# Eight edge products instead of four behind the aggregation loop of a graph network on one Trainium2 core

## The chip, the core and the metric

The program runs on one core of a Trainium2 chip. A core has five engines that run side by side and wait for each other through semaphores: TensorE (PE, matmuls), VectorE (DVE), ScalarE (ACT), GpSimd (POOL) and SyncE (SP), which issues most of the transfers. All transfers of the core are carried by its 16 DMA engines. The metric is the device time of one execution in microseconds (us). A "tile" is 128 rows of 512 float32 values, 256 KB.

## The reference

Two graph layers with residual and layer norm, on 10,000 nodes of 512 features and 5,000 edges that are sorted by their target node. Only the first layer and the edge term of the second bear on the change:

```python
# layer 0: x is scaled by 1/sqrt(degree) at the source and summed over the edges of each target
norm = dinv[src] * dinv[dst]
H = X @ W
msgs = H[src] * norm[:, None]
out = jax.ops.segment_sum(msgs, dst, num_segments=N) + b
x = _layernorm(x + leaky(out))
...
# layer 1: needs, for each edge, a product of its own attributes with one third of Wr
x_cat = jnp.concatenate([node_feat[src], node_feat[dst], edge_feat], axis=-1)
r = x_cat @ Wr.T + br
```

The kernel sums `dinv[src] * x[src]` over each target's edges first and multiplies by W afterwards. The part `edge_feat @ Wr_edge` depends on nothing of layer 0, so its 40 tile products can stand anywhere ahead of layer 1.

## The kernel before

Edges are cut into 40 tiles (`ET = 40`) of 128. The program is written out in three stages, and the order of the instructions on each engine is the order of its own `..._program` function. There is no scheduler.

**The prologue stage** holds two jobs that share the engines.

The *aggregation* goes over the 40 edge tiles in `NB = 20` turns of two tiles, 2j and 2j+1. For one tile t:
POOL gathers the 128 source rows of x (`x_of`, line 541, into `node_sum`) and their factors (`dinv_of`, line 541, into `dinv_src`); it may run four tiles ahead, since `x_of(t)` waits until tile t-4 has been scaled. ACT scales them (`scale_rows`, line 460, into `acc_x` or `acc_xx`). PE transposes the tile into PSUM (`turn_x`, line 618, four matmuls). DVE runs a segmented prefix sum along the edges (`scan`, line 706, four instructions, into `node_x`). PE transposes back (`turn_back`, line 625), one turn later. ACT scales by the target's factor into one of only two buffers (`sum_rows`, line 466, `sum_y` for even and `sum_xx` for odd tiles), and SP stores it (`store_sums`, line 350, into `sum_table`). `sum_rows(t)` waits until the store of tile t-2 has landed.

The *edge products* are 40 products `edge_part(t)` of 12 matmuls of 128x512 each (lines 208 to 210: float32 as a sum of high and low parts). Their input is loaded by SP (`load_ea`, line 339, four slots), rounded by ACT (`high`, line 449, `ea_hi`), and the rest is taken by DVE (`low`, line 698, `ea_lo`); ACT copies the result out (`part_rows`, line 454, four buffers `part`), and SP stores it (`store_part`, line 346, `edge_part`). The first 11 (`PRE = 11`) stand ahead of the aggregation. `ahead(j)` deals out the rest: 25 to the 20 turns, one to each turn but two to turns 3, 7, 11, 15 and 19, and the last four (`LATE = 4`) behind the loop, in what the code calls turn `j == NB`. Of these four the first stands ahead of the last two `turn_back`, and three behind them.

In a turn PE does `turn_x`, `turn_x`, `edge_part(one)`, `turn_back`, `edge_part(two)` if there is a second, `turn_back`. ACT scales the tiles of the turn after, then `high`, `part_rows`, `sum_rows`. DVE does `scan(2j)`, `low` of the next turn's first edge tile, `scan(2j+1)`, `low` of the next turn's second if there is one. In turns 0 to 5 ACT and DVE also split a half of a later weight each (`weights_high`, line 444, `weights_low`, line 694).

**The node stage** computes layer 0 for 79 node tiles. Before its first tile POOL gathers rows of `sum_table` (line 591, once the last sums have landed), DVE adds them to x (line 1017, `node_agg`), PE transposes (line 1046), writes four banks whole (`open_banks`, line 1028, which waits until all 40 edge parts have been copied out of PSUM), ACT puts the bias into a bank (line 961), ACT and DVE split the transposed tile (lines 945 and 988), and PE multiplies by W (lines 208 to 210 with `agg_hi`, `agg_lo`). From there on one node tile follows another. **The edge stage** and a last stage follow.

The turn behind the loop on SP, before the change:

```python
if j == NB:
    store_sums(2 * j - 2)
    store_sums(2 * j - 1)
    for i in range(R):
        if i == 0:
            sp.wait_ge(back_ok, ET)
        sp.dma_start(g.node_x[:, i, :], g.x[i * P:(i + 1) * P, :])
    for t in ahead(j):
        store_part(t)
    for i in range(R, 2 * R):
        sp.dma_start(g.node_x[:, i, :], ...)
```

Of the kernel before, what the change touches and what calls it, by code (L numbers as in the profile page):

```python
# [263 lines left out]
def prologue_stage(nc, g):  # L264
# [4 lines left out]
    R = 4  # L269
    RP = 4  # L270
    PRE = 11
    LATE = 4
    with ExitStack() as ctx:
        ix = g.index
        run = g.node_x[:, 0:R, :].rearrange("p r (k e) -> p r k e", k=K)
# [59 lines left out]
    def sync_program(sp):  # L335
# [72 lines left out]
        for j in range(NB + 1):  # L408
            one, two = first_and_second(j)
            next_one, next_two = first_and_second(j + 1)  # L410
            if j == NB:
                store_sums(2 * j - 2)
                store_sums(2 * j - 1)
                for i in range(R):
                    if i == 0:
                        sp.wait_ge(back_ok, ET)
                    sp.dma_start(g.node_x[:, i, :], g.x[i * P:(i + 1) * P, :]).then_inc(g.node_in[i], 16)
# [3 lines that stand above are left out]
                    sp.dma_start(g.node_x[:, i, :], g.x[i * P:(i + 1) * P, :]).then_inc(g.node_in[i], 16)  # L421
                continue
            for t in next_one:
                load_ea(t + R)
            if j + 6 < EARLY:
                load_weights(j + 6)
            for t in one:
                store_part(t)
            if j >= 1:
                store_sums(2 * j - 2)  # L430
            for t in next_two:
                load_ea(t + R)
            for t in two:
                store_part(t)
            if j >= 1:
                store_sums(2 * j - 1)

    def scalar_program(act):
        def weights_high(i):
            if i < 2:  # L440
                act.wait_ge(w_in[(0, 4)[i]], 16)
            else:
                act.wait_ge(w_in[i // 2], 32)
            nc.scalar.copy(g.w_half(g.w_hi, i), g.w_half(g.over_lo, i)).then_inc(w_hi_ok, 1)

        def high(t):
            act.wait_ge(ea_in[t % R], 16 * (t // R + 1))
            wait(act, r_mm, t - R + 1)
            nc.scalar.copy(ea_hi[:, t % R, :, :], ea_cols[:, t % R, :, :]).then_inc(ea_hi_ok, 1)

        def part_rows(t):
            act.wait_ge(r_mm, t + 1)
            wait(act, part_out[t % RP], 16 * (t // RP))
            nc.scalar.copy(part[:, t % RP, :], ps_r[t % 2][:]).then_inc(part_ok, 1)

        def scale_rows(t):
            if t < ET:
                act.wait_ge(x_in[t % R], 32 * (t // R + 1))
                wait(act, x_t, t - 1)
                nc.scalar.activation(scaled[t % 2][:], x_rows[:, t % R, :], ACT.Copy, scale=dinv_src[:, t % R, :]).then_inc(scaled_ok, 1)  # L460

        def sum_rows(t):
            act.wait_ge(back_ok, t + 1)
            act.wait_ge(deg_step, DINV_DST)
            wait(act, row_out[t % 2], 16 * (t // 2))
            nc.scalar.activation(sums[t % 2][:], ps_back[t % 2][:], ACT.Copy, scale=dinv_dst[:, t:t + 1]).then_inc(row_ok, 1)

        for i in range(2):
            g.load_half(act, g.w_half(g.over_lo, i), i).then_inc(w_in[(0, 4)[i]], 16)
            act.dma_start(ea_tile(i), g.ea[i * P:(i + 1) * P, :]).then_inc(ea_in[i], 16)  # L470
        act.wait_ge(const_ok, EPSILON)
        nc.scalar.activation(deg[:, 1, 0:1], g.eps[:], ACT.Sqrt)
        weights_high(0)
        high(0)
        weights_high(1)
        for t in range(1, 4):
            high(t)
        part_rows(0)
        high(4)
        high(5)  # L480
        part_rows(1)
        part_rows(2)
        part_rows(3)
        high(6)
        act.wait_ge(const_ok, IDENTITY)
        act.wait_ge(index_step, CNT)
        nc.scalar.activation(ix.small[:, 0, :], ix.cnt[:], ACT.Sqrt, bias=g.ones[:, 0:1]).then_inc(index_step, 1)
        part_rows(4)
        high(7)
        part_rows(5)  # L490
        high(8)
        part_rows(6)
        act.wait_ge(deg_step, DEGREES)
        nc.scalar.activation(deg[:, 1, :], deg[:, 0, :], ACT.Sqrt).then_inc(deg_step, 1)
        high(9)
        part_rows(7)
        part_rows(8)
        high(10)
        high(11)
        scale_rows(0)  # L500
        scale_rows(1)
        part_rows(9)
        part_rows(10)
        for t in ahead(0):
            if t > 11:
                high(t)
        for j in range(NB + 1):
            one, two = first_and_second(j)
            next_one, next_two = first_and_second(j + 1)
            if j == NB:  # L510
                first, second, third, fourth = ahead(j)
                part_rows(first)
                sum_rows(2 * j - 2)
                sum_rows(2 * j - 1)
                high(third)
                part_rows(second)
                high(fourth)
                part_rows(third)
                part_rows(fourth)
                continue  # L520
            scale_rows(2 * j + 2)
            scale_rows(2 * j + 3)
            for t in next_one:
                high(t)
            for t in one:
                part_rows(t)
            if j >= 1:
                sum_rows(2 * j - 2)
            for t in next_two:
                high(t)  # L530
            for t in two:
                part_rows(t)
            if j >= 1:
                sum_rows(2 * j - 1)
            if j + 2 < EARLY:
                weights_high(j + 2)
# [57 lines left out]
    def tensor_program(pe):  # L594
# [63 lines left out]
        for j in range(NB + 1):  # L658
            one, two = first_and_second(j)
            next_one, next_two = first_and_second(j + 1)  # L660
            if j == NB:
                first, second, third, fourth = ahead(j)
                edge_part(first)
                turn_back(2 * j - 2)
                turn_back(2 * j - 1)
                edge_part(second)
                edge_part(third)
                edge_part(fourth)
                continue
            turn_x(2 * j)  # L670
            turn_x(2 * j + 1)
            for t in one:
                edge_part(t)
            if j >= 1:
                turn_back(2 * j - 2)
            for t in two:
                edge_part(t)
            if j >= 1:
                turn_back(2 * j - 1)
# [1133 lines left out]
def finish_stage(nc, g):  # L1813
# [8 lines left out]
    STATS, PAIRED = 2, 4  # L1822
    LATE = 4
    with ExitStack() as ctx:
# [289 lines left out]
```

## Time and profile before

| | |
|---|---|
| median of three runs | 1360.38 us (1358.02 to 1360.54) |
| the profiled execution | 1361.24 us, of which its span is 1359.5 us |
| PE busy in the span | 1278.2 us (94%) |
| DVE, ACT, POOL busy | 1078.5, 637.5, 812.1 us |
| mean DMA rate | 190 GB/s |
| aggregation loop | from 45.1 to about 168.7 us |
| last edge product ends, first node product starts | 180.5 us, 188.3 us |

Each row of the timeline below gives the start, the length, engine, line, operation, output<-inputs and shape. A bracket at its end is the idle time of that engine just before it and what ended it. Lengths of matmuls are modelled and overlap: the pace is told by their starts. The chain of work that ended last, as the page prints it, covers only the last part of the span and doesn't reach the stretch that is changed; it is read from timelines, waits and windows.

### The profile page before, as it was taken

The page shows a single profiled execution, that of the slowest core. Times are in us where ns is not written, and L with a number is a line of the kernel's source. Part 1 is how long each engine was busy: PE and PEld are TensorE (multiplying, and loading weights), DVE is VectorE, ACT ScalarE, POOL GpSimd, SP SyncE. Part 2 cuts the span into 40 slices and gives each one's busy share as a digit, 9 for nine tenths or more (in the row PEclk, how much of TensorE's full clock was granted, in tenths as well). Part 3 has the DMA queues.
Part 4 walks back from the last instruction along what each step waited for, and adds up shares of the span by engine and source line. Part 5 has one row for each costly group of instructions (what it writes and reads, how often), then busy time and mean ns, then how long its engine had stood idle before and what let it go on. Part 6 is the DMA issues. An engine that isn't in the chain of part 4 may idle for free. (4 is left out here: it accounts for less than half of the span.)

```text
span 1359.5 us, 21821 instructions
## 1 busy us (share of the span) xinstructions
PE 1278.2 (94%) x6374; PEld 1028.1 (76%) x6374; DVE 1078.5 (79%) x2074; ACT 637.5 (47%) x1243; POOL 812.1 (60%) x752
## 2 busy tenths in 40 slices
PE   7889989999999699999999999999999999859887
PEld 5677778888888588888888888888888888644333
DVE  7476649999999226888888889888888888957877
ACT  3576647888887212233322332233222333246877
POOL 3566346767675443556666666666666664367775
PEclk9899999999999799999999999999999999879999
DMA  8888767888885514444444444444444443839886
GB/s 285 279 271 281 261 217 260 255 263 269 264 257 186 178 47 110 140 141 140 118 123 119 125 127 127 129 127 137 140 133 132 138 139 100 297 133 355 276 282 227
DMA packets 128300, 257.95 MB, mean 190 GB/s; under 512 B 21459, under 2 KB 21907, under 8 KB 128114
## 3 DMA queue, kind: packets, MB, share of 16 engines
q1 hardware_dynamic: 97490, 175.31, 39.2%
q0 software_dynamic: 29920, 80.38, 20.4%
q10 hardware_dynamic: 832, 1.57, 0.3%
q8 instruction: 26, 0.43, 0.1%
q14 instruction: 32, 0.26, 0.1%
HBM read 197.18 MB, written 73.60 MB: 199 GB/s over the span
## 5 line engine op out<-in xcount | busy, mean ns | idle before, releaser
L208 PE MATMUL ps<-w_lo,w_hi 128*128 128x512 f32 (+2 forms) x1140 | 415.5, 365 | 4.3 <-DVE w_lo L1477 1.5
L209 PE MATMUL ps<-w_hi,w_lo 128*128 128x512 f32 (+2 forms) x1140 | 410.0, 360 | 0.0
L210 PE MATMUL ps<-w_hi 128*128 128x512 f32 (+2 forms) x1140 | 409.8, 359 | 0.0
L208 PEld LDWEIGHTS ps<-w_lo,w_hi 128*128 128x128 f32 x1140 | 217.0, 190 | 36.9 <-DVE w_lo L1477 2.7
L210 PEld LDWEIGHTS ps<-w_hi 128*128 128x128 f32 x1140 | 216.6, 190 | 32.1
L209 PEld LDWEIGHTS ps<-w_hi,w_lo 128*128 128x128 f32 x1140 | 217.2, 191 | 29.6
L1261 POOL TENSOR_TENSOR acc_x<-acc_x,node_rows 128x512 f32<-128x512 f32 x72 | 117.4, 1631 | 80.7 <-DMA node_rows<-x_table 76.4
L919 POOL TENSOR_TENSOR node_y<-node_z,node_x 128x512 f32<-128x512 f32 x79 | 102.7, 1300 | 72.3 <-DVE node_agg L1017 37.8
L208 PE MATMUL ps<-w_lo,agg_hi 128*128 128x512 f32 x316 | 132.0, 418 | 1.2 <-DVE agg_lo L988 1.2
L210 PE MATMUL ps<-w_hi,agg_hi 128*128 128x512 f32 x316 | 125.1, 396 | 0.0
L209 PE MATMUL ps<-w_hi,agg_lo 128*128 128x512 f32 x316 | 124.5, 394 | 0.0
L1463 DVE TENSOR_TENSOR_SCAN v_turned<-coef_all,carry,v_turned 128x256 f32<-128x256 f32 x76 | 110.5, 1509 | 0.7
L1221 POOL DMA_INDIRECT edge_rows<-x_table,edge_gather_idx x72 | 80.1, 1113 | 42.1 <-POOL edge_gather_idx L1217 28.5
L1922 POOL DMA_INDIRECT rows_over_w_lo<-msg_table,last_edge x79 | 80.1, 1014 | 31.0 <-ACT rows_over_w_lo L1977 17.1
L1352 ACT CAST w_hi<-v_turned 128x1024 fp32r<-128x1024 f32 x17 | 17.9, 1051 | 158.4 <-DVE v_turned L1463 158.4
L1487 DVE TENSOR_TENSOR k_rows<-ps,bk_row 128x512 f32<-128x512 f32 x40 | 27.5, 690 | 72.7 <-PE ps L210 72.7
L923 POOL DMA_INDIRECT node_sum<-sum_table,last_edge x75 | 72.5, 967 | 17.4 <-DVE node_agg L1017 5.9
L1375 ACT ACTIVATE v_turned<-ps,bv_col 128x256 f32<-128x256 f32 x76 | 29.9, 476 | 94.8 <-PE ps L210 94.8
L1244 POOL TENSOR_TENSOR k_rows<-k_rows,q_rows 128x512 f32<-128x512 f32 x38 | 49.2, 1295 | 40.2 <-DVE k_rows L1487 39.8
L939 ACT COPY node_z<-ps 128x512 f32<-128x512 f32 x79 | 46.4, 587 | 52.7 <-PE ps L210 52.7
L210 PEld LDWEIGHTS ps<-w_hi,agg_hi 128*128 128x128 f32 x316 | 59.7, 189 | 14.7
L208 PE MATMUL ps<-w_lo,ea_hi 128*128 128x512 f32 x160 | 67.2, 420 | 3.6 <-DVE ea_lo L698 3.6
(271 smaller groups left out, 2842.4 us busy)
## 6 DMA issues: line engine op xcount, KB each, us to landing
node_x<-in_x SPq DMA_DIRECT2D x79, 256.0 KB, 4.1
x_table<-node_x SPq DMA_DIRECT2D x79, 256.0 KB, 2.4
node_rows<-x_table SPq DMA_DIRECT2D x79, 256.0 KB, 8.3
coef_all<-coef_table SPq DMA_DIRECT2D x38, 512.0 KB, 7.1
edge_part<-part SPq DMA_DIRECT2D x40, 256.0 KB, 4.6
out_dram<-rows_over_w_lo SPq DMA_DIRECT2D x40, 256.0 KB, 5.9
node_x<-in_ea SPq DMA_DIRECT2D x38, 256.0 KB, 4.5
msg_table<-dst_rows_and_msg SPq DMA_DIRECT2D x38, 256.0 KB, 4.8
```

What stands on the lines that cost most here:

```text
L208: pe.matmul(to, left[0], right[1], start=first, stop=False, skip_group_check=onto)
L209: pe.matmul(to, left[1], right[0], start=False, stop=False, skip_group_check=onto)
L210: return pe.matmul(to, left[0], right[0], start=False, stop=last, skip_group_check=onto)
L919: nc.gpsimd.tensor_tensor(y[:, i % RY, :], z[:, i % 2, :], xr[:, i % RX, :], ALU.add).then_inc(y_ok, 1)
L923: nc.gpsimd.indirect_dma_start(out=rn[:, t % RS, :], out_offset=None, in_=g.sum_table, in_offset=bass.IndirectOffsetOnAxis(ap=g.last_edge[ ...
L939: nc.scalar.copy(z[:, q, :], ps_o[(s - 6) % 4][:]).then_inc(z_ok, 1)
L1221: nc.gpsimd.indirect_dma_start(out=rows[:, q, o, :], out_offset=None, in_=g.x1_table, in_offset=bass.IndirectOffsetOnAxis(ap=at, axis=0)). ...
L1244: nc.gpsimd.tensor_tensor(k_rows[:, q, :], k_rows[:, q, :], q_rows[:, q, :], ALU.mult).then_inc(qk_ok, 1)
L1261: nc.gpsimd.tensor_tensor(g.acc_x[r, :], g.acc_x[r, :], node[r, q, :], ALU.add).then_inc(x_added, 1)
L1375: nc.scalar.activation(vt[:, (s - 1) % 2, m, :], two(ps_r)[m // 2][:, m % 2, :], ACT.Identity, bias=g.bv_col[:, m:m + 1]).then_inc(v_ok, 1)
L1463: v.tensor_tensor_scan(vt[:, s, m, :], coef[:, m, 0, :], vt[:, s, m, :], carry[:, m:m + 1], ALU.mult, ALU.add).then_inc(scan_ok, 1)
L1922: nc.gpsimd.indirect_dma_start(out=u(k), out_offset=None, in_=g.msg_table, in_offset=bass.IndirectOffsetOnAxis(ap=g.last_edge[:, k:k + 1], ...
```

## The change

`LATE` goes from 4 to 8. `ahead(j)` then deals 21 edge products to the 20 turns: one to each but turn 19, which has two. The other eight stand behind the loop, tiles 32 to 39: the first ahead of the last two `turn_back`, seven behind them. What the code did for four named tiles it now does in a loop over any number; and since the last two inputs (tiles 38 and 39) are no longer loaded within the loop, SP loads them behind the last two stores of sums, ahead of the first node rows.

```diff
-    LATE = 4
+    LATE = 8
...
                 store_sums(2 * j - 2)
                 store_sums(2 * j - 1)
+                for t in ahead(j)[2:]:
+                    load_ea(t + R)
                 for i in range(R):
                     if i == 0:
                         sp.wait_ge(back_ok, ET)
...
-                first, second, third, fourth = ahead(j)
-                part_rows(first)
+                last = ahead(j)
+                part_rows(last[0])
                 sum_rows(2 * j - 2)
                 sum_rows(2 * j - 1)
-                high(third)
-                part_rows(second)
-                high(fourth)
-                part_rows(third)
-                part_rows(fourth)
+                for t in last[2:]:
+                    high(t)
+                    part_rows(t - 1)
+                part_rows(last[-1])
...
-                first, second, third, fourth = ahead(j)
-                edge_part(first)
+                last = ahead(j)
+                edge_part(last[0])
                 turn_back(2 * j - 2)
                 turn_back(2 * j - 1)
-                edge_part(second)
-                edge_part(third)
-                edge_part(fourth)
+                for t in last[1:]:
+                    edge_part(t)
```

How it moves instructions. First DVE, from the end of turn 5 to the end of turn 7, before (`w_lo` is a weight half, `node_x<-goes_on` a scan of one tile, `ea_lo` the low part of an edge tile):

```order
L694 TENSOR_TENSOR w_lo<-rows_over_w_lo,w_hi 128x1024
L706 SCALAR_TENSOR_TENSOR node_x<-goes_on,node_x,ps2 128x128 x4
L698 TENSOR_TENSOR ea_lo<-node_x,ea_hi 128x512
L706 SCALAR_TENSOR_TENSOR node_x<-goes_on,node_x,ps3 128x128 x4
L698 TENSOR_TENSOR ea_lo<-node_x,ea_hi 128x512
L706 SCALAR_TENSOR_TENSOR node_x<-goes_on,node_x,ps2 128x128 x4
L698 TENSOR_TENSOR ea_lo<-node_x,ea_hi 128x512
L706 SCALAR_TENSOR_TENSOR node_x<-goes_on,node_x,ps3 128x128 x4
```

and the same place in the changed kernel:

```order
L694 TENSOR_TENSOR w_lo<-rows_over_w_lo,w_hi 128x1024
L706 SCALAR_TENSOR_TENSOR node_x<-goes_on,node_x,ps2 128x128 x4
L698 TENSOR_TENSOR ea_lo<-node_x,ea_hi 128x512
L706 SCALAR_TENSOR_TENSOR node_x<-goes_on,node_x,ps3 128x128 x4
L706 SCALAR_TENSOR_TENSOR node_x<-goes_on,node_x,ps2 128x128 x4
L698 TENSOR_TENSOR ea_lo<-node_x,ea_hi 128x512
L706 SCALAR_TENSOR_TENSOR node_x<-goes_on,node_x,ps3 128x128 x4
```

The low part of turn 7's second edge tile is gone from between the scans. The same goes for its `high` and `part_rows` on ACT, its load and its store on SP, and its product on PE, and for turns 3, 11 and 15.

Second SP, from the end of turn 19 to the last loads of the first node rows, before:

```order
L346 DMA edge_part<-part 128x512
L350 DMA sum_table<-sum_xx 128x512
L350 DMA sum_table<-sum_y 128x512
L350 DMA sum_table<-sum_xx 128x512
L417 DMA node_x<-in_x 128x512 x4
L346 DMA edge_part<-part 128x512 x4
L421 DMA node_x<-in_x 128x512 x4
```

and in the changed kernel, where two of the lines have moved down by two:

```order
L346 DMA edge_part<-part 128x512
L350 DMA sum_table<-sum_xx 128x512
L350 DMA sum_table<-sum_y 128x512
L350 DMA sum_table<-sum_xx 128x512
L339 DMA node_x<-in_ea 128x512 x2
L419 DMA node_x<-in_x 128x512 x4
L346 DMA edge_part<-part 128x512 x8
L423 DMA node_x<-in_x 128x512 x4
```

Two loads now stand ahead of the first four node rows, and eight stores of edge parts instead of four between these and the next four.

Third ACT behind the loop, before, from the copy of edge part 36 to the bias of the first node tile:

```order
L454 COPY part<-ps6 128x512
L466 ACTIVATE sum_y<-ps4,dinv_dst 128x512
L466 ACTIVATE sum_xx<-ps5,dinv_dst 128x512
L449 CAST ea_hi<-node_x 128x512
L454 COPY part<-ps7 128x512
L449 CAST ea_hi<-node_x 128x512
L454 COPY part<-ps6 128x512
L454 COPY part<-ps7 128x512
L961 COPY ps4<-b_row 128x512
```

and in the changed kernel the first half of the same stretch, from the copy of edge part 32 on:

```order
L456 COPY part<-ps6 128x512
L468 ACTIVATE sum_y<-ps4,dinv_dst 128x512
L468 ACTIVATE sum_xx<-ps5,dinv_dst 128x512
L451 CAST ea_hi<-node_x 128x512
L456 COPY part<-ps7 128x512
L451 CAST ea_hi<-node_x 128x512
L456 COPY part<-ps6 128x512
L451 CAST ea_hi<-node_x 128x512
L456 COPY part<-ps7 128x512
```

The pair of a `high` and a `part_rows` now comes six times instead of twice before the last copy. The first node tile's bias stands behind all of them, as it did.

## Rows read from the trace of the kernel before

**Rows 1.** Windows: the node stage from 200 us, PE busy first after the span.

```profile
200.00:225.00 25.00, 25.00 (x126) 20.48 (x125) 22.00 (x54) 17.82 (x37) 17.05 (x16) 1.00 0.70 231
```

**Rows 2.** Windows: PE, PEld, DVE, ACT, POOL busy; clock, DMA share, GB/s.

```profile
137.38:146.24 8.86, 7.44 (x42) 6.14 (x41) 6.26 (x15) 5.15 (x10) 6.82 (x7) 1.00 0.97 299
...
99.33:160.71 61.38, 56.44 (x334) 47.73 (x333) 41.80 (x99) 41.21 (x71) 34.98 (x36) 1.00 0.88 286
45.05:168.65 123.60, 108.18 (x614) 90.68 (x612) 85.52 (x192) 80.51 (x134) 70.37 (x72) 0.97 0.85 273
```

**Rows 3.** Waits between 50 and 160 us: total, times, longest.

```profile
POOL node_sum L541 <- ACT acc_x L460: 18.9, 10, 5.0
...
ACT sum_y L466 <- DMA sum_table<-sum_y: 8.2, 9, 2.8
```

**Rows 4.** Timeline of POOL: gathers issued without a wait.

```profile
45.12 0.95 POOL L541 DMA_INDIRECT node_sum<-in_x,edge_idx  x1 [0.30 <-ACT acc_xx L460]
...
64.08 0.94 POOL L541 DMA_INDIRECT dinv_src<-dinv_table,edge_idx  x1 [0.30 <-issue]
```

**Rows 5.** Timeline of POOL: the gathers of x that waited, tiles 22 to 38.

```profile
101.15 0.94 POOL L541 DMA_INDIRECT node_sum<-in_x,edge_idx  x1 [2.50 <-ACT acc_x L460]
...
113.37 0.94 POOL L541 DMA_INDIRECT node_sum<-in_x,edge_idx  x1 [2.34 <-ACT acc_x L460]
...
148.06 0.95 POOL L541 DMA_INDIRECT node_sum<-in_x,edge_idx  x1 [2.01 <-ACT acc_x L460]
```

**Rows 6.** Timeline of ACT: turns 3, 7 and 10, ahead of scaling.

```profile
73.50 1.04 ACT L444 CAST w_hi<-rows_over_w_lo 128x1024 fp32r<-128x1024 f32 x1
...
99.09 0.59 ACT L454 COPY part<-ps 128x512 f32<-128x512 f32 x1 [1.93 <-PE ps L210]
...
111.22 0.69 ACT L466 ACTIVATE sum_y<-ps,dinv_dst 128x512 f32<-128x512 f32 x1 [2.82 <-DMA sum_table<-sum_y]
```

**Rows 7.** DMA between 99.33 and 160.71 us: queues, then issues with median landing.

```profile
q1 hardware_dynamic: 6879, 12.51, 57.4%
q0 software_dynamic: 2142, 5.00, 30.4%
...
edge_part<-part SPq DMA_DIRECT2D x14, 256.0 KB, 4.1
node_x<-in_ea SPq DMA_DIRECT2D x13, 256.0 KB, 4.3
sum_table<-sum_xx SPq DMA_DIRECT2D x11, 256.0 KB
sum_table<-sum_y SPq DMA_DIRECT2D x10, 256.0 KB, 4.8
```

**Rows 8.** Timeline of PE: one edge product in the loop, then behind it.

```profile
142.97 0.47 PE L208 MATMUL ps<-w_lo,ea_hi 128*128 128x512 f32 x1
...
145.81 0.60 PE L625 MATMUL ps<-ident,node_x 128*128 128x128 f32 x4
...
171.48 1.03 PE L625 MATMUL ps<-ident,node_x 128*128 128x128 f32 x8
...
180.31 0.39 PE L210 MATMUL ps<-w_hi,ea_hi 128*128 128x512 f32 x1
183.50 1.11 PE L1046 MATMUL ps<-ident,node_agg 128*128 128x128 f32 x4 [2.80 <-DVE node_agg L1017]
184.27 2.06 PE L1028 MATMUL ps<-w_hi 128*128 128x512 f32 x4
...
188.30 0.50 PE L208 MATMUL ps<-w_lo,agg_hi 128*128 128x512 f32 x1 [1.18 <-DVE agg_lo L988]
```

**Rows 9.** Timeline of ACT behind the loop.

```profile
180.74 0.59 ACT L454 COPY part<-ps 128x512 f32<-128x512 f32 x1 [2.13 <-PE ps L210]
186.41 0.59 ACT L961 COPY ps<-b_row 128x512 f32<-128x512 f32 x1 [5.09 <-PE ps L1028]
```

**Rows 10.** The tile edge_part: time from issue to landing of its stores.

```profile
DMA to landing us min/median/max: 2.0/5.3/10.2
```

## The prediction

> **What bounds the kernel now.** I read the windows first, since the printed chain ends before this stretch. Behind the prologue the node stage keeps PE busy for the whole of every window [rows 1], so whatever the prologue saves or costs until the first node product comes through at full size. In the loop, from 45.1 to 168.7 us, no engine is full: PE is busy 108.2 of 123.6 us, and the DMA engines have a share of 0.85, over turns 8 to 18 of 0.88 [rows 2]. The reader should see a loop of 20 turns of 6.2 us in which three things come out almost alike.
>
> Next the waits. The largest is POOL's, for tiles that ACT has not scaled yet, 18.9 us in ten waits; ACT waits 8.2 us for its buffer `sum_y`, whose store has not landed [rows 3]. POOL's timeline says what a turn costs if nothing holds POOL: 16 gathers start at 45.12 and end 64.08 + 1.24 later, 20.2 us, so 1.26 us each and 5.05 us for the four of a turn [rows 4]. PE's says what a turn costs PE: one edge product takes 142.97 to 145.81, 2.84 us [rows 8], and the sixteen transposes about 1.75 us, at 0.11 each; together 4.6 us, or 7.4 us with two products. So turns with one product run at PE's pace and eat the gathers that lie ready, and a turn with two holds ACT until its end. Then POOL waits: tile 22's gather waited 2.50 us behind turn 7, whose second copy was at 99.09 [rows 5, 6], and tile 38's 2.01 us behind turn 15. Tile 26's 2.34 us had another cause: ACT had waited 2.82 us for the store of `sum_y` [rows 5, 6].
>
> Behind the loop PE ends its transposes at about 172.4, does three edge products of 2.72 us (to 180.54) and then has nothing: the first node rows reach it at 183.50, 11.1 us after the transposes, and the first node product starts at 188.30 [rows 8].
>
> **The change, part by part.** All work is kept; PE, ACT, DVE and SP do the same number of instructions. What counts is where PE and the DMA engines stood idle.
>
> *Added behind the loop:* four products of 2.72 us, (180.54 - 172.4)/3 [rows 8]: **+10.9 us**.
>
> *The gap ahead of the node stage closes.* Now 180.54 to 188.30, 7.8 us. With seven products behind the transposes (19.0 us) the node rows, ready after 11.1 us, are there long before. What is left is a chain that no earlier data shortens: the last part copy starts 0.2 us after the last matmul and takes 0.59 [rows 9], the four bank matmuls wait for it and take 0.23 each, ending some 1.8 us after the last product; ACT's bias follows, and from its start to the first product it was 186.41 to 188.30, 1.9 us [rows 8, 9]. Sum 3.8 us with the step between: **-3.9 us**. Lower bound: only the 3.0 us until 183.50 go.
>
> *SP's queue behind the loop.* Moved past it are the loads of tiles 38 and 39. The second waits until `low(35)`, which stands behind the copy of part 33, about 4.6 us after the transposes; queued behind it are the four loads of node rows and then all part stores. The node rows would start to load 3 us later, and are needed 19 us after the transposes: nothing. The store of part 32 would start about 7 us after them, and lands 5.3 us later by the median [rows 10], at 12.4. ACT's copy of part 36 needs that buffer, and wants it at 11.1; queued behind this copy are `high(38)` and so PE's product 38, which could start at 13.6. Copy, cast and low part take 1.7 us: it starts at 14.1. **+0.5 us**; nothing if stores land in under 4.8 us, 5 us if like the slowest, 10.2 us [rows 10].
>
> *The loop.* Four products go, so PE could give back 11 us; but PE isn't the only limit. I follow POOL's gathers, because the loop ends a fixed time behind the last. Up to tile 22's: the 2.5 us wait behind turn 7's second product goes, but for the 0.3 us that stand before every gather, 2.2 us. Turn 3's second product sits in a chain in which ACT's and DVE's weight halves already set the pace (ACT splits one at 73.50, right behind that turn's last sum [rows 6]); the `high` and the copy that go are worth some 1.2 us. So 3.4 us up to there. From tile 22's gather (101.15) to tile 38's (148.06) there are eight turns in 46.9 us, 5.86 each [rows 5]. What would one cost with one product each? POOL alone: 5.05. The DMA engines: in turns 8 to 18 the plain queue took 0.574 of 61.38 us for 48 transfers, 0.73 us each, and the gathers' queue 0.304 for 18 tiles, 1.04 us each [rows 2, 7]. A turn with one product is four plain transfers and two tiles of gathers: 2.9 + 2.1 = 5.0 us at a full share. The highest share over a stretch here is 0.97, over a long one 0.88 [rows 2]. At 0.97 a turn takes 5.15 us, at 0.88 5.7. I take 0.95, between them and nearer to the busy stretch, since the load becomes even: 5.25. Eight turns are 42.0 us, 4.9 us less. Turn 19 keeps its two products. Together **-8.3 us**; bounds 3.4 + 46.9 - 8 x 5.7 = 4.7, and with turns at POOL's 5.05, 9.9 us.
>
> Sum: 10.9 - 3.9 + 0.5 - 8.3 = **-0.8 us**. The profiled execution of 1361.24 us (span 1359.5) would become 1360.4; it lies 0.9 us over the median of 1360.38, so the median becomes **1359.6 us**.
>
> Weighed against a page: the rows say that the DMA engines are nearly full at 286 GB/s [rows 2]. The Trainium skill (DMA: Bandwidth & Descriptors, Specifications) gives a limit of some 358 GB/s to one core; six tiles of a turn, 1.57 MB, would by that take 4.4 us, an estimate, so DMA would bind nothing and the turn be POOL's.
>
> **The rivals.** Less than 0.2% (2.7 us) either way cannot be told from no change.
>
> *Faster: the turns come down to POOL's pace.* [...] Then the loop gives 9.9 us. POOL's ten waits are 18.9 us, 5.0 the longest, in turn 3 [rows 3]; the five from tile 22 on (the first, second and last in [rows 5]) are 9.9; the other four, 4.0 us, or 2.8 over the fixed 0.3 each, lie in turns 4 to 7. If they go as well, it is 12.7. The sum is -2.4 to -5.2, say -4: 1356.4 us. For it: POOL's waits are by far the largest, and all ten end with ACT. Against it: DMA share 0.97 already over turn 15.
>
> *Slower: two sum buffers hold the turn.* `sum_rows(t)` waits for the store of t-2, which is exactly one turn earlier. A turn is then copy 0.69 + issue 0.2 + landing. At the median landing of 4.8 us [rows 7] that is 5.7 us; the loop gives 3.4 + 46.9 - 45.6 = 4.7, and the sum is +2.8. At 5.3, the median of the part stores [rows 10], it is 6.2 us a turn, the loop gives 0.7 and the sum is +6.8: about 1365 us in the middle. It decides from a landing of 4.8 us on. For it: the 2.82 us wait of this kind fell into turns at 4.6 us, the densest of the loop [rows 6]. Against it: landing of `sum_y` was shorter in other turns, and ACT waited for it in only 9 of 20. The Trainium skill (DMA: Bandwidth & Descriptors, Latency and other measured facts) says that HBM access goes from 0.2 us to 2 us at high load; the turns being denser, this rule speaks for this rival.
>
> *Slower: a ring behind the loop.* A part store that takes 9 us to land, near the slowest of 10.2 [rows 10], holds product 38 for 4.2 us instead of 0.5: +2.9, 1363.3 us. It decides from there.
>
> *Slower: the gap stays.* If the node stage's start costs 7.5 us even with its rows ready, because its transposes and bank matmuls run as slowly as now (2.06 us for the four [rows 8]) and its first gathers queue, 3.7 us less are saved: +2.9, 1363.3 us.
>
> **How the numbers follow.** Likeliest, DMA and POOL together: 0.45, by itself 1357.8 to 1362. POOL's pace: 0.27. Sum buffers: 0.17. Ring: 0.06. Gap: 0.05. The range leaves out the lower tail of the second case and the upper of the third: 1355.5 to 1364.5. Faster by over 0.2% is most of the POOL case and a bit of the first, 0.30; slower is most of the last three, 0.26; within 0.2%, 0.44.
>
> **What would show it.** The turns' starts on PE (first transpose of each): about 5.2 us apart from turn 8 to 18, with no 8 to 10 us turn left but 19; 5.05 means POOL alone, 5.7 the sum buffers, and then ACT's wait for `sum_table` stores rises over 10 us. POOL's waits for ACT fall from 18.9 to under 9 us. Tile 39's last transposes at about 164 us instead of 172.4. From there 19 to 20 us to the last edge product's end, with one wait of PE of 0.5 us ahead of product 38 or none, and from that end 3.8 us to the first node product. The prediction is wrong if the loop gives under 5 or over 11 us, or if something far behind, in the node or edge stage, moves by more than the shift.

## The result, and the profile after

| | before | after |
|---|---|---|
| median of 8 runs each, same chip | 1360.18 us (1356.03 to 1362.61) | 1366.82 us (1363.78 to 1371.75) |
| ratio | | 1.0061, 95% interval 1.0044 to 1.0078 |
| the profiled execution (span) | 1361.24 us (1359.5) | 1368.84 us (1367.0) |

The change makes the kernel slower, by 8.3 us by the ratio and 6.6 by the two medians. Differences between kernels are given below as differences of such ratios, in per cent, with the microseconds that this share of 1360 us makes. The forecast was 1359.6 us with a range up to 1364.5: wrong, on the slow side.

Busy times of the changed kernel, from its page:

```profile
PE 1282.8 (94%) x6374; PEld 1032.1 (75%) x6374; DVE 1079.4 (79%) x2074; ACT 638.2 (47%) x1243; POOL 814.2 (60%) x752
```

DVE, ACT and POOL have stayed within 2.1 us; PE has 4.6 us more for the same work, so some of its matmuls have become longer. The windows of the whole loop and of turns 8 to 18 (columns as in [rows 2]), and of a stretch behind the loop that had no such row before:

```profile
44.88:163.70 118.82, 102.57 (x578) 85.65 (x577) 82.94 (x188) 77.78 (x126) 71.92 (x72) 0.96 0.86 275
95.06:153.26 58.20, 51.45 (x310) 43.30 (x309) 41.62 (x100) 40.12 (x66) 37.24 (x39) 1.00 0.90 292
183.02:188.00 4.98, 4.98 (x13) 3.93 (x14) 2.02 (x3) 0.23 (x1) 2.16 (x2) 0.54 0.39 125
```

In this trace the loop has done what was said: turns 8 to 18 take 58.20 / 11 = 5.29 us each (before 61.38 / 11 = 5.58), at DMA share 0.90. The third row is the surprise: 5 us of matmuls at a granted clock of 0.54 (0.50, the lower of the clock's two levels of 1.2 and 2.4 GHz, until 187.45, and full from there). What is ahead of it stands in the timeline of PE behind the loop:

```profile
163.70 1.03 PE L626 MATMUL ps<-ident,node_x 128*128 128x128 f32 x8
...
177.97 0.39 PE L210 MATMUL ps<-w_hi,ea_hi 128*128 128x512 f32 x1
183.02 0.79 PE L208 MATMUL ps<-w_lo,ea_hi 128*128 128x512 f32 x1 [4.66 <-DVE ea_lo L698]
183.61 0.63 PE L209 MATMUL ps<-w_hi,ea_lo 128*128 128x512 f32 x1
...
187.77 0.39 PE L210 MATMUL ps<-w_hi,ea_hi 128*128 128x512 f32 x1
...
190.53 0.39 PE L210 MATMUL ps<-w_hi,ea_hi 128*128 128x512 f32 x1
190.76 0.60 PE L1046 MATMUL ps<-ident,node_agg 128*128 128x128 f32 x4
...
191.68 1.16 PE L1028 MATMUL ps<-w_hi 128*128 128x512 f32 x4 [0.33 <-ACT part L456]
...
194.82 0.50 PE L208 MATMUL ps<-w_lo,agg_hi 128*128 128x512 f32 x1 [1.54 <-DVE agg_lo L988]
```

The transposes end at 164.6, 7.8 us earlier than the 172.4 of before. Five products follow without a gap (to 178.2). Then PE has nothing for 4.8 us (178.2 to 183.02), and product 38 behind this (183.02 to 188.0) takes 5.0 us instead of 2.72. From the last product to the first node product it is 4.1 us, in place of 7.8 ([rows 8] has the same places before). DVE is named as PE's releaser, but it had waited for ACT. Its timeline, at the copy of part 36:

```profile
172.96 0.59 ACT L456 COPY part<-ps 128x512 f32<-128x512 f32 x1 [1.61 <-PE ps L210]
...
181.14 0.58 ACT L456 COPY part<-ps 128x512 f32<-128x512 f32 x1 [7.07 <-DMA edge_part<-part]
...
182.62 0.63 ACT L451 CAST ea_hi<-node_x 128x512 fp32r<-128x512 f32 x1
```

The copy waited 7.07 us for the store of part 32 to land and free its buffer, and the cast for product 38 (182.62) stands two copies behind. Third, SP's queue, and the DMA issues between 164 and 184 us with their median landing:

```profile
165.67 0.32 SPq L350 DMA_DIRECT2D sum_table<-sum_xx  x1
166.91 2.81 SPq L339 DMA_DIRECT2D node_x<-in_ea  x2
169.76 1.86 SPq L419 DMA_DIRECT2D node_x<-in_x  x4
171.66 20.22 SPq L346 DMA_DIRECT2D edge_part<-part  x8
```

```profile
edge_part<-part SPq DMA_DIRECT2D x6, 256.0 KB, 9.4
node_x<-in_x SPq DMA_DIRECT2D x4, 256.0 KB, 7.6
node_x<-in_ea SPq DMA_DIRECT2D x2, 256.0 KB, 3.0
node_sum<-sum_table,last_edge POOLq DMA_INDIRECT x4
```

Part 32's store is issued at 171.66, 7.1 us after the transposes, as the prediction had it. It stands right behind a megabyte of node rows and lands after 9.4 us, not after 5.3 [rows 10]. Its place alone doesn't explain this, because the kernel before has stores in the same place, right behind the four loads of node rows, and they landed after 5.3 us. The queue of SP, POOL's first gather of `sum_table`, and the stores' median landing, in the kernel before:

```profile
174.03 1.89 SPq L417 DMA_DIRECT2D node_x<-in_x  x4
175.97 5.70 SPq L346 DMA_DIRECT2D edge_part<-part  x4
...
176.59 1.35 POOL L591 DMA_INDIRECT node_sum<-sum_table,last_edge  x1 [23.65 <-DMA sum_table<-sum_xx]
...
edge_part<-part SPq DMA_DIRECT2D x4, 256.0 KB, 5.3
```

and POOL's first gather in the changed kernel:

```profile
168.54 0.95 POOL L592 DMA_INDIRECT node_sum<-sum_table,last_edge  x1 [22.84 <-DMA sum_table<-sum_xx]
```

Before, the loads of node rows start 1.6 us after the transposes and 2.6 us ahead of the gathers, and land after 3.2 us by the median. Now they stand behind the loads of tiles 38 and 39, start 5.2 us after the transposes and 1.2 us behind the first gather, and land after 7.6 us. The part stores come behind these later and longer loads.

Last, the waits between 50 and 160 us, answering to [rows 3]:

```profile
ACT sum_y L468 <- DMA sum_table<-sum_y: 11.5, 11, 2.2
...
POOL node_sum L542 <- ACT acc_x L462: 9.1, 6, 3.0
...
ACT sum_xx L468 <- DMA sum_table<-sum_xx: 1.8, 3, 0.6
```

POOL's waits for ACT have halved, from 18.9 to 9.1 us. ACT's waits for row sums that haven't landed have gone from 11.2 (8.2 of them for `sum_y`) to 13.3 us.

In this one trace the difference at the first node product is 194.82 - 188.30 = 6.5 us: -7.8 loop, +10.9 products, +7.1 ring wait (4.8 idle and 2.3 in the slow product), -3.7 gap. Another 1.0 us comes behind it, in code that the change doesn't touch.

### The profile page after: what moved, and what is told of

Its sections match the earlier page's. It is cut to its first block and busy times, and to the rows that moved or that the text cites. A ratio compares the mean times of both kernels' runs of the same rounds, so it can differ in the third digit from the quotient of the medians.

```text
span 1367.0 us, 21821 instructions
## 1 busy us (share of the span) xinstructions
PE 1282.8 (94%) x6374; PEld 1032.1 (75%) x6374; DVE 1079.4 (79%) x2074; ACT 638.2 (47%) x1243; POOL 814.2 (60%) x752
```

## The experiments

Each kernel was timed against the kernel before on its own chip; what each run expects was put down ahead of it. All but the sixth compute what the kernel before computes. "Theory" is at first that the ring of part buffers behind the loop costs the time. The loop on its engines is the same in the change and in experiments 1 and 2, and yet its length differs from trace to trace; so one trace is no measure of it.

### 1. Three part stores ahead of the node rows (a_first8)

```diff
-                for t in ahead(j)[2:]:
-                    load_ea(t + R)
+                last = ahead(j)
+                for i in range(3):
+                    store_part(last[i])
+                    if i + 2 < len(last):
+                        load_ea(last[i + 2] + R)
+                for t in last[5:]:
+                    load_ea(t + R)
                 for i in range(R):
...
-                for t in ahead(j):
+                for t in last[3:]:
                     store_part(t)
```

> The changed kernel (eight products behind the loop), but SP issues the stores of parts 32, 33 and 34 right behind the last sums, ahead of the four loads of node rows, not behind them; all work is kept. Theory (the ring of four part buffers): in the changed kernel the store of part 32 was issued 7 us behind the last transposes and took 9.4 us to land, ACT's copy of part 36 waited 7.1 us for it, PE stood idle for 4.8 us and then ran product 38 at half clock, 2.3 us more. Here the store is issued 5 us earlier, so both go: 7.1 us less than the changed kernel, about 1359.7 us, no wait of PE between the last transposes and the last edge product, 19.0 us between them. Rival (the DMA engines are simply full behind the loop): another transfer comes late in its place, the stretch stays above 23 us and the time above 1363.5 us.

Measured: 1362.55 us against 1359.37, ratio 1.0021 (1.0008 to 1.0034). The queue of SP and the landings between 160 and 182 us:

```profile
167.81 0.32 SPq L350 DMA_DIRECT2D sum_table<-sum_xx  x1
168.18 0.46 SPq L346 DMA_DIRECT2D edge_part<-part  x1
...
173.35 2.02 SPq L424 DMA_DIRECT2D node_x<-in_x  x4
```

```profile
edge_part<-part SPq DMA_DIRECT2D x8, 256.0 KB, 3.0
node_x<-in_x SPq DMA_DIRECT2D x4, 256.0 KB, 6.8
```

The eight stores of this stretch land after 3.0 us by the median; the three that were moved, at 168.18, 170.27 and 172.99, after 2.5, 2.3 and 4.8 us. PE runs through: the window from the transposes to the last product is busy throughout, at full clock.

```profile
166.70:185.60 18.90, 18.90 (x86) 15.64 (x85) 5.48 (x8) 7.71 (x14) 5.78 (x6) 1.00 0.79 265
```

That is seven products of 2.70 us. The order of one queue is worth 1.0061 - 1.0021 = 0.40%, or 5.4 us. But this kernel is still 0.21% (2.9 us) slower than before, where about 1359.7 us was expected.

### 2. Six part buffers instead of four, order as in the change (b_ring6)

```diff
-    RP = 4
+    RP = 6
...
-                    for out in g.part_out:
-                        act.wait_ge(out, 16 * ET // len(g.part_out))
+                    for i, out in enumerate(g.part_out):
+                        act.wait_ge(out, 16 * ((ET - 1 - i) // len(g.part_out) + 1))
```

> The changed kernel, with six part buffers instead of four and the order of all transfers as in the change; all work is kept. Theory (the ring): the copy of part 36 needs no landed store any more, and parts 38 and 39 need those of 32 and 33 only 16.5 us behind the last transposes, when they have just landed. 6 to 7 us less than the changed kernel, about 1360 us; the stores themselves still take 9 us to land. Rival (order and load of the transfers, not the ring): PE waits for something else in the same place, and less than 2 us are gained. A third one: the six buffers also help in the loop, whose transposes then end well ahead of the 164.6 us of the changed kernel.

Measured: 1358.73 us against 1359.37, ratio 1.0003 (0.9985 to 1.0021). No engine waits for a part store any more, though they land as late as in the changed kernel (6.5 us by the median over the run, 2.1 to 9.6; 6.4 in the change). With a different cure for the same wait the cost goes too: the ring is shown twice. But here 0.58%, or 7.9 us, go, and nothing is left over the kernel before that its interval could tell from zero. The last transposes and the first node product show where experiments 1 and 2 differ:

```profile
161.22 1.03 PE L626 MATMUL ps<-ident,node_x 128*128 128x128 f32 x8
...
185.23 0.50 PE L208 MATMUL ps<-w_lo,agg_hi 128*128 128x512 f32 x1 [1.54 <-DVE agg_lo L988]
```

The transposes end at 162.1, 2.5 us earlier than in the change and 4.6 earlier than in experiment 1; behind them both take the same time, 23.1 us. That is the third rival of the expectation, and it stays open. In the changed kernel no engine waited for a part store ahead of 164 us, so the six buffers had no wait to take away in the loop, and the three traces (164.6, 166.7, 162.1) may just show how much a loop with the same code varies.

### 3. and 4. Fewer products behind the loop (c_first6, d_first5)

Experiment 1 with `LATE = 6` and two stores ahead of the node rows, and with `LATE = 5` and one.

> Six products behind the loop instead of eight or four (turns with two edge products are then three), and the stores of the first two of their parts ahead of the loads of node rows; all work is kept. Theory: the loop gives 2 us for each product that leaves it, so its transposes end near 168.4 us (172.4 in the kernel before), five products of 2.72 us follow, and 3.9 us later the first node product starts: 185.9 us instead of 188.3, 2.4 us less than the kernel before, about 1357.8 us. Rival (nothing is won as long as a turn with two products is left, since POOL and ACT still wait behind it): the transposes end past 171 us, and the time is 1360.5 us or more.

> Five products behind the loop, four of them behind the last transposes, and the store of the first one's part ahead of the loads of node rows; all work is kept. Theory: the node rows are ready 11.1 us behind the last transposes and four products take 10.9 us, so this is the least number that closes the gap. Transposes end near 170.4 us, the first node product starts 15 us later, 185.4 us: 2.9 us less than the kernel before, about 1357.3 us. Rival (the loop gives nothing for one product): transposes end at 172 us, the time is 1359 us.

Measured: 1361.21 against 1359.37, ratio 1.001 (0.9997 to 1.0024), and 1363.05, ratio 1.0025 (1.0009 to 1.0042). Both miss the gain that was expected. In the trace of the second the first node product is at 186.52, 3.3 us ahead of experiment 1's, but the stretch from POOL's last four gathers of edge rows (its line 1317) to the end took 206.6 us against 203.2. So with two sum buffers the number of products behind the loop hardly shows between 5 and 8. What the 3.4 us at the end are, these traces don't tell.

### 5. The weight halves six turns later (f_wlate8)

In the loop of the change turn 4 takes 9.0 us at a granted clock of 0.62 (turn 3 takes 6.6, turn 5 takes 4.9), and it stands next to the splitting of later weights. I took that for the rest of the loss.

```diff
-            if j + 2 < EARLY:
-                weights_high(j + 2)
+            if 2 <= j - 6 < EARLY:
+                weights_high(j - 6)
```

(and `weights_low` likewise), on top of experiment 1.

> As a_first8 (eight products behind the loop, the first three part stores ahead of the node rows), but ACT and DVE split the six weight halves in turns 8 to 13 instead of 0 to 5; all work is kept. Theory: in the changed kernel, a_first8 and both kernels with five and six late products, turn 4 took 7.7 to 10.5 us, because turn 3 has lost its second product while weight halves stand between the scans: PE is idle for some 3.5 us and then runs a product at half clock. Without weight halves turns 3 and 4 take about 5 us each and turns 8 to 13 about 5.7: loop 3 us shorter than in a_first8, time about 1359.5 us. Rival (the gathers' landing, not the weights, opens the gap in turn 3): turn 4 or 3 stays above 7 us, the time stays at 1362.5 us.

Measured: 1365.87 against 1358.27, ratio 1.0059 (1.0037 to 1.008). Turn 4 still takes 9.1 us without any weight half beside it, at clock 0.81:

```profile
65.30:74.40 9.10, 6.37 (x31) 5.22 (x30) 5.98 (x14) 5.25 (x10) 6.82 (x8) 0.81 0.89 292
```

Turn 3 is down to 4.5 us, so the two together are shorter than in experiment 1 (13.5 against 16.8 us). But turns 8 to 13, which have the halves now, take 37.1 us for 31.5, and the kernel is 0.38% slower than experiment 1. Turn 4 doesn't hang on the halves, and moving them costs more than it frees.

### 6. Less input (h_light)

```diff
-                sp.dma_start(ea_tile(t % R), g.ea[t * P:(t + 1) * P, :])
+                n = P // 8 if 15 <= t < 36 else P
+                sp.dma_start(ea_tile(t % R)[0:n, :], g.ea[t * P:t * P + n, :])
```

> As a_first8, but the loads of edge inputs 15 to 35 bring 16 rows of 128 (the products of those tiles use what the slot held before). One of the six large transfers of each turn is gone. Theory (DMA engines are one of the limits in the loop): landing times fall from 4.5 to under 4 us and the turns 8 to 18 come to 5.05 us, POOL's pace, from 5.25; the loop ends 2 to 4 us earlier, time about 1359.5 us. Rival (POOL alone, or the chain from ACT over DVE to PE): turns stay as in a_first8 and the time within 1 us of it.

Measured: 1356.93 against 1358.27, ratio 0.9991 (0.9976 to 1.0007): 0.30% or 4 us less than experiment 1. DMA share over turns 8 to 18 falls from 0.91 to 0.79, but in the trace (an execution 3.9 us over this kernel's median) these turns take 57.50 / 11 = 5.23 us, as in experiment 1 (5.25):

```profile
93.40:150.90 57.50, 51.31 (x311) 43.30 (x310) 40.88 (x98) 39.54 (x67) 37.72 (x39) 1.00 0.79 249
```

The stores of row sums still land after 4.2 us by the median, and ACT still waits 11.2 us for them. So some 4 us hang on the load by the ratios, with intervals that nearly touch, but a lower DMA share alone didn't shorten the turns of this trace. What waits for the row sums was next.

### 7. The second product of turn 3 kept (g_turn3)

Experiment 1 with turn 3 given two products again, and seven behind the loop.

> As a_first8, but turn 3 keeps its second edge product and seven are left behind the loop; all work is kept. Theory (clock): with the product in turn 3 PE has no long gap there, turn 3 takes 7.2 us and turn 4 5.5 us at full clock, as in the kernel before, 12.7 us together instead of 15.6 (the changed kernel) or 16.8 (a_first8). Loop end no later than in a_first8, one product less behind it: 2.7 to 4 us less than a_first8, about 1359 us. Rival (half clock there is chance and has nothing to do with turn 3): turns 3 and 4 together take 15 us here too, and the time is 1362 us.

Measured: 1361.66 against 1358.27, ratio 1.0018 (1.0006 to 1.0031). The clock is 1.00 throughout turns 3 and 4, and the two take 15.9 us all the same (15.6 in the change): PE filled with products, or idle and then slow, these two turns take the same. Turn 2 ahead of them took 5.4 us in this trace and 8.5 and 9.7 in experiment 1 and the change, so turn 4 ends 3.7 us earlier; but the time doesn't show it (0.03% less than experiment 1, with one product less behind the loop). So a full clock in turns 3 and 4 brought nothing that these intervals can see. What makes turns 2 to 4 long or short isn't shown.

### 8. Four buffers for the row sums (e_sums4)

Experiment 1, with `sum_y`, `sum_xx` and two more used in turn:

(Left out are the store, which takes the same buffer, and the later waits, which now count four semaphores instead of two.)

```diff
-        scaled, sums = [g.acc_x, g.acc_xx], [g.sum_y, g.sum_xx]
+        more_sums = sb(ctx, "more_sums", [P, 2, D])
+        scaled, sums = [g.acc_x, g.acc_xx], [g.sum_y, g.sum_xx, more_sums[:, 0, :], more_sums[:, 1, :]]
...
-            wait(act, row_out[t % 2], 16 * (t // 2))
-            nc.scalar.activation(sums[t % 2][:], ps_back[t % 2][:], ACT.Copy, scale=dinv_dst[:, t:t + 1]).then_inc(row_ok, 1)
+            wait(act, row_out[t % 4], 16 * (t // 4))
+            nc.scalar.activation(sums[t % 4][:], ps_back[t % 2][:], ACT.Copy, scale=dinv_dst[:, t:t + 1]).then_inc(row_ok, 1)
```

> As a_first8, with four buffers for the row sums instead of two; all work is kept. Theory (in the loop DMA engines and POOL set the turn): ACT's waits for landed sums, 15 us in a_first8 between 50 and 160 us, go, but the turns 8 to 18 stay at 5.2 to 5.3 us, and the time falls by less than 1.5 us. Rival (the two sum buffers hold the turn): the turns come down to 5.05 us or less, the loop ends 2 to 3 us earlier, time about 1360 us.

Measured: 1356.13 against 1358.27, ratio 0.9984 (0.9972 to 0.9996): 0.37% or 5.0 us less than experiment 1, where I had expected under 1.5. ACT waits for no row-sum store any more, and POOL waits for ACT twice (8 times and 10.1 us in experiment 1). The wait of POOL, then the window of turns 8 to 18:

```profile
POOL node_sum L548 <- ACT acc_x L468: 2.6, 2, 2.3
```

```profile
91.60:146.60 55.00, 50.73 (x310) 43.28 (x309) 41.34 (x99) 39.51 (x67) 36.99 (x39) 1.00 0.92 308
```

Turns of 5.00 us, at a DMA share of 0.92 and 308 GB/s. So it is the landing of the row sums that held the turn, and 5.25 us was no limit of the DMA engines.

### 9. to 12. The four buffers with and without the change

The kernel before with four sum buffers (i_before_sums4); the changed kernel with them and nothing else (j_sums4_only); experiment 8 with five products behind the loop and one store ahead (k_sums4_late5), and with six and two (l_sums4_late6).

> The kernel before (four products behind the loop), with four buffers for the row sums instead of two; all work is kept. Theory (the sum buffers hold turns with one product, the second products hold the others): ACT's 11 us of waits for landed sums go, but POOL's waits behind turns 3, 7, 11 and 15, some 2 us each, and PE's 7.4 us in these turns stay. The loop gives 3 to 4 us, transposes end at 169 us, time 3 us less than the kernel before, about 1355.5 us. Rival (PE and POOL set this loop, the waits for sums lie beside them): within 1 us of the kernel before.

> The changed kernel with four buffers for the row sums instead of two, and nothing else; all work is kept. It differs from e_sums4 by the order of the part stores behind the loop alone. Theory (the ring of part buffers costs 7 us behind the loop): loop as in e_sums4, transposes end near 158 us, then 26 us to the last edge product's end with one wait of PE of 4 to 5 us ahead of product 38, and the time is 6 to 7 us over e_sums4, about 1362.5 us. Rival (the wait came from a late loop or from the two sum stores ahead of it): under 3 us over e_sums4.

> Four buffers for the row sums, five products behind the loop, the first one's part store ahead of the node rows; all work is kept. Theory: with the sums out of the way POOL's 5.05 us and PE's 6.0 us a turn (24 products in 20 turns: 20 x 1.75 + 24 x 2.84 = 103 us) are about level; transposes end 3 to 5 us later than in e_sums4, at 162 us, and three products of 2.72 us less follow: first node product at 177 us instead of 181.3, time 4 us under e_sums4, about 1352 us. Rival (each product put back costs the loop its full length, and the two turns behind it more): transposes end at 167 us or later, no gain over e_sums4.

> Four buffers for the row sums, six products behind the loop, the first two part stores ahead of the node rows; all work is kept. Theory: 20 x 1.75 + 23 x 2.84 = 100 us for PE, just under POOL's 101; transposes end near 160.5 us, two products less than in e_sums4 follow: first node product at 178.3, 3 us under e_sums4, about 1353 us. Rival: as for five products; transposes end past 164 us, no gain over e_sums4.

| four sum buffers and | median (before 1359.27, but 1358.27 for e) | ratio | 95% interval |
|---|---|---|---|
| the kernel before (i) | 1352.92 us | 0.9959 | 0.9942 to 0.9976 |
| the change, its order (j) | 1362.07 us | 1.0024 | 1.001 to 1.0039 |
| the change, three stores first (e) | 1356.13 us | 0.9984 | 0.9972 to 0.9996 |
| five late, one store first (k) | 1352.5 us* | 0.9952 | 0.9935 to 0.9969 |
| six late, two stores first (l) | 1353.04 us | 0.995 | 0.993 to 0.9969 |

\* One of k's twelve executions took 3276.69 us. It is counted in this median (1351.35 without it), but not in the ratio.

The times came out as expected for j, k and l (within 1 us) and 2.6 us lower than expected for i. The ring wait came back in j as it was in the change, by ACT's and PE's timelines:

```profile
176.92 0.59 ACT L457 COPY part<-ps 128x512 f32<-128x512 f32 x1 [7.02 <-DMA edge_part<-part]
```

```profile
178.80 0.79 PE L208 MATMUL ps<-w_lo,ea_hi 128*128 128x512 f32 x1 [4.61 <-DVE ea_lo L699]
```

j and e differ by the order of SP's queue alone: 0.40%, 5.4 us, the same as between the change and experiment 1. And i shows what the kernel before does with that wait gone; three rows of its PE: the last transposes of the loop, the node stage's first, and its first product.

```profile
162.14 1.04 PE L626 MATMUL ps<-ident,node_x 128*128 128x128 f32 x8
...
173.96 0.66 PE L1047 MATMUL ps<-ident,node_agg 128*128 128x128 f32 x4 [2.60 <-DVE node_agg L1018]
...
177.53 0.50 PE L208 MATMUL ps<-w_lo,agg_hi 128*128 128x512 f32 x1 [1.54 <-DVE agg_lo L989]
```

Against that, e's transposes end 4.9 us earlier (158.1 against 163.0), but its first node product is at 181.25, 3.7 us later; the ratios say 0.25%, 3.4 us. Here trace and ratios agree, and the change in its best order loses because the loop (4.9 us) and the closed gap (6.3 to 4.1 us) return less than the four products cost. The versions with most behind the loop are the slower ones; i, k and l can't be told apart, and are the fastest here, 0.4 to 0.5% under the kernel before.

## Why the prediction was wrong

**The failed step: "+0.5 us" for SP's queue behind the loop.** The store's issue (7.1 us after the transposes), the buffer it frees and the chain from there to product 38 were as written. What failed is the landing, taken at 5.3 us, and with it the "nothing" for node rows that start to load 3 us later. They are indeed not needed until 19 us after the transposes, but loaded that late they have POOL's gathers beside them from the start, and the first part store behind them lands after 9.4 us. The 5.3 fitted the kernel before, not only as the median of all 40 stores but at this very place in the queue; the change altered what is under way at that place. In j the first of these stores took 9.3 us again, in experiment 2, where nobody waits for it, 8.8. How much of the delay is due to the gathers, and how much to the finished parts that go out together, no run separates. And the slow product wasn't in the term at all: PE idle for 4.8 us, then product 38 at clock 0.54, 2.3 us more. Together it is +7.1 instead of +0.5 in the trace; by the ratios 5.4 between the change and experiment 1 and between j and e, and 7.9 between the change and experiment 2. It was the third rival, "a ring behind the loop", which put a landing of 9 us at 4.2 us of waiting (+2.9 in all) and was given 0.06. Shown by undoing it in two ways (experiments 1 and 2) and by its return in j.

**The loop: "-8.3 us".** Its size isn't settled. With the ring's cost gone, the loop returns what is missing to the four products and the closed gap: 10.9 - 3.7 - 2.9 = 4.3 us by experiment 1 (2.6 to 6.1 by its interval) and 10.9 - 3.7 - 0.4 = 6.8 us by experiment 2 (4.3 to 9.2). With four sum buffers on both sides it is 4.9 in the traces. The traces of the same loop say 7.8 (the change), 5.7 (experiment 1) and 10.3 (experiment 2) against 172.4 of the one trace before. So it is about 4 to 7, in the lower part of the predicted bounds (4.7 to 9.9) or just under; that the one trace of the change came within 0.5 us of the forecast is luck as much as working. In turns 8 to 18 it shows 5.29 us for 5.25, nearly as predicted. Which turns vary stays open: those between 2 and 7 differ by microseconds from trace to trace of kernels with the same loop, and experiments 5 and 7, which were to find a loss there, gained nothing.

**What sets a turn: rival "two sum buffers", right in mechanism, wrong in place.** I had put a turn down to DMA share. Experiment 6 took share away and the turn stayed at 5.23 in its trace; experiment 8 took ACT's wait away and it fell to 5.00, about POOL's pace of 5.05 [rows 4], at a higher share. But the wait holds the kernel before just as much: four buffers give it 0.41%, the changed one 0.37%. So it explains the length of the turns, not the difference that was to be forecast. The Trainium skill (DMA: Bandwidth & Descriptors, Specifications) gives some 358 GB/s to one core, which made DMA no bound here; experiment 8's 308 GB/s with POOL at its pace agrees, and over 4.8 us (183.5 to 188.3) the kernel before moved 369 GB/s, more than the page gives. The Trainium skill's rule of longer latency at high load (same page, Latency and other measured facts) spoke for longer landings in the denser turns; the traces show none, 4.3 us by the median for the row sums after and 4.5 before. The landing was long enough already.

**Right:** four products cost 10.9 (four of 2.70 to 2.72). The gap closes by 3.7 for 3.9, to 4.1 us. In i, though, the gap was 6.3 us, its bank matmuls not slowed behind 2.6 us of idle time, so this term is nearer 2.2 where the clock stays up. POOL's waits were to fall under 9 us and fell to 9.1, a near miss. "The gap stays" didn't happen.

**The size as a whole:** -0.8 forecast. With the ring's 5.4 us and the 4.9 us that the loop returned between i and e, it is 10.9 - 3.7 + 5.4 - 4.9 = +7.7, against 8.3 by the ratio (6.0 to 10.6). With experiment 2's figures the ring is larger and the loop returns more. The step of 1.0 us far behind the change is within what the stretch at the end differs by between kernels (203.2 to 206.6 us), unexplained.

## What to carry to other kernels

Work that is put behind a loop to hide a latency is free only up to that latency: here 11.1 us, four products, and each one more must be paid back in full by the loop. If it runs through a ring of buffers that a DMA frees, count the landing with all that is under way by then, ahead of it in the queue and beside it from other engines. A median over the run misses that, and so does the same place in the kernel before, once the change has moved its neighbours. Put stores that somebody waits for ahead of prefetches that nobody needs yet. A buffer that is reused once a turn wants a turn longer than its copy, the issue and the landing together, or a second pair: here that was worth 0.4% in either kernel.

## What the hardware showed that was not expected

A store of 256 KB landed in 2.5 us ahead of the four loads of node rows (experiment 1) and in 9.4 us behind them (the change), but in 5.3 us behind them in the kernel before, where they ran ahead of the gathers. After 4.8 us without work PE had 5 us of matmuls at a granted clock of 0.54, so a wait cost half as much again (2.3 us). After gaps of 3.0 and 2.8 us the same bank matmuls were slow in the kernel before (2.06 us for four [rows 8], at clock 0.50) and at full clock in i. DMA engines held 308 GB/s over 55 us at a share of 0.92, with transfers and gathers mixed.
